# Paged attention: heads 0 and 4 of a batch scored in full precision, heads 1, 2, 3, 5, 6 and 7 in three rounded products

## The reference, cut to what matters

```
B, S, D, HQ, HK = 32, 32, 128, 32, 8      # batches, tokens, head size, query heads, key heads
kc = k_cache[block_table].reshape(B, 512, HK, D)     # 16 pages of 32 keys a batch
k_all = concatenate([kc, k], axis=1)                 # 544 keys
scores = einsum('bqhd,bkhd->bhqk', q, repeat(k_all, HQ // HK, axis=2)) * D ** -0.5
scores = where(valid, scores, -1e30)
o = einsum('bhqk,bkhd->bqhd', softmax(scores), repeat(v_all, HQ // HK, axis=2))
```

## Time and profile before

| | us |
|---|---|
| median of 3 runs (1693.58 to 1695.39) | 1694.57 |
| the profiled execution, its own time | 1689.82 |
| its span, first to last instruction | 1687.6 |
| of it the paged attention, from the first scores to the last values | about 859 to 1475 |

### The profile page before, as it was taken

The page is one execution under the profiler, slowest core; times in us unless marked ns, Lnnn a source line. Parts: engine busy times, 40 slices in busy tenths (PEclk is TensorE's granted clock), DMA queues, the critical chain, the costliest instruction groups (busy, mean ns, idle before and its releaser), DMA issues. The chain is left out here.

```text
span 1687.6 us, 34168 instructions
## 1 busy us (share of the span) xinstructions
PE 1619.2 (96%) x10792; PEld 1404.1 (83%) x10792; DVE 1104.5 (65%) x2942; ACT 943.1 (56%) x2392; POOL 369.9 (22%) x370
## 2 busy tenths in 40 slices
PE   2899999999999999999979999999999999999998
PEld 2787888888888788888869999999999999977777
DVE  8405543454436657777768888888888888864443
ACT  3224323232222266766669989998899888822221
POOL 1000000000000246656532332223222322122210
PEclk9999999999999999999979999999999999999999
DMA  6621121110110433443578889988998898594301
GB/s 231 206 91 52 65 69 68 68 44 24 68 63 26 162 107 107 134 134 106 156 268 277 282 297 300 305 287 286 304 302 295 273 301 299 184 325 140 122 12 50
DMA packets 239311, 290.69 MB, mean 172 GB/s; under 512 B 18682, under 2 KB 182938, under 8 KB 239258
## 3 DMA queue, kind: packets, MB, share of 16 engines
q1 hardware_dynamic: 220826, 222.89, 39.8%
q0 software_dynamic: 18432, 67.12, 12.3%
HBM read 237.43 MB, written 50.41 MB: 171 GB/s over the span
## 5 line engine op out<-in xcount | busy, mean ns | idle before, releaser
L1591 PE MATMUL p_val<-probs_t,vals 128*128 128x128 f32 x2048 | 271.7, 276 | 1.7 <-DMA vals<-in_v_pages,rows_now 1.7
L1591 PEld LDWEIGHTS p_val<-probs_t,vals 128*128 128x128 f32 x2048 | 249.3, 192 | 2.0 <-DMA vals<-in_v_pages,rows_now 2.0
L1501 DVE CUSTOM_DVE_ANT_0 probs<-p_score,mask 128x544 f32<-128x544 f32 x256 | 184.3, 720 | 80.2 <-issue 77.6
L1406 ACT ACTIVATE probs<-probs,low 128x544 f32<-128x544 f32 x256 | 190.6, 745 | 0.3 <-DVE low L1501 0.3
L1060 POOL TENSOR_TENSOR w_lo<-w_raw,w_hi 128x512 fp32r<-128x512 f32 x44 | 57.7, 1316 | 548.4 <-DVE w_hi L1098 531.9
L1414 ACT ACTIVATE probs_t<-p_turn 128x512 f32<-128x512 f32 x256 | 149.5, 584 | 50.6 <-PE p_turn L1570 46.6
L450 PE MATMUL p_score<-wo_hi,q_hi 128*128 128x288 f32 x448 | 153.4, 342 | 11.9 <-DVE low L1501 11.3
L1490 DVE TENSOR_TENSOR wo_lo<-keys,wo_hi 128x544 fp32r<-128x544 f32 x224 | 161.7, 722 | 0.7 <-issue 0.7
L450 PE MATMUL p_tile<-w_hi,y_hi 128*128 128x512 f32 x384 | 156.9, 409 | 2.4 <-PEq L463 2.4
L1570 PE MATMUL p_turn<-cst,probs 128*128 128x128 f32 x1024 | 154.8, 274 | 3.2 <-issue 1.5
L1401 ACT ACTIVATE wo_hi<-keys 128x544 fp32r<-128x544 f32 x224 | 146.1, 652 | 17.6 <-PE p_score L452 12.9
(11 more groups left out here) (216 smaller groups left out, 3604.4 us busy)
## 6 DMA issues: line engine op xcount, KB each, us to landing
keys<-in_k_pages SPq DMA_DIRECT2D x512, 128.0 KB
qk_new<-x_res SPq DMA_DIRECT2D x80, 256.0 KB, 2.3
x_res<-qk_new SPq DMA_DIRECT2D x32, 512.0 KB
o_new<-x_res SPq DMA_DIRECT2D x32, 512.0 KB
w_raw<-in_w_vkq_t SPq DMA_DIRECT2D x12, 1024.0 KB, 5.6
w_raw<-in_w_qkv_t SPq DMA_DIRECT2D x10, 1024.0 KB, 8.2
toep<-kpad SPq DMA_DIRECT2D x32, 256.0 KB, 4.9
w_raw<-in_w_dense_t SPq DMA_DIRECT2D x8, 1024.0 KB, 5.3
```

The lines of the kernel that those rows point to most:

```text
L1406: nc.scalar.activation(probs[:, i % 8, :], probs[:, i % 8, :], ACT.Exp, bias=low[:, i % 4:i % 4 + 1], scale=-1.0, accum_out=total[:, i % 4 ...
L1501: v.tensor_tensor_reduce(out=probs[:, i % 8, :], in0=score_at(i % 2, slice(0, KEYS)), in1=mask[:, i // HK, :], scale=1.0, scalar=3e38, op0 ...
L1591: mm = pe.matmul(p_val[:, h, half * P:(half + 1) * P], vals[:, slot, c, k * D:(k + 1) * D], probs_t[:, i % 2, c, :], start=(c == 0 and hal ...
```

## The change

Head 4 of every batch is treated as head 0 is: `PLAIN = (0, HK // 2)`. `split_hi` and `split_lo` return at once for it, PE takes its scores in two full-precision matmuls from `queries` and `keys`, and doesn't wait for `q_lo` or `k_lo` there. The second piece of the queries, now 384 columns for heads 5 to 7, is split at k = 5. A batch has six splits where it had seven, and `splits_to` counts accordingly.

```diff
--- before.py
+++ after.py
@@ -1305,9 +1305,10 @@
         score_at = lambda n, part: p_score[:, FROM[n] + part.start:FROM[n] + part.stop]
         half_heads = lambda a, slot, n: a[:, slot, n * HQ * S // 2:(n + 1) * HQ * S // 2]
 
-        QUERY_AT = {1: slice(P, HQ * S // 2), HK // 2: slice(HQ * S // 2, HQ * S)}
-        SPLITS = HK - 1
-        splits_to = lambda m, i: 2 * SPLITS * m + i // HK * SPLITS + i % HK
+        PLAIN = (0, HK // 2)
+        QUERY_AT = {1: slice(P, HQ * S // 2), HK // 2 + 1: slice(HQ * S // 2 + P, HQ * S)}
+        SPLITS = HK - len(PLAIN)
+        splits_to = lambda m, i: 2 * SPLITS * m + i // HK * SPLITS + i % HK - (i % HK > HK // 2)
         both = lambda body, eng: (body(0, True), _loop(eng, 1, B // 2, lambda m: body(m, False)))
 
         block = ctx.enter_context(nc.Block())
@@ -1390,7 +1391,7 @@
             def split_hi(m, i):
                 r = m * RB + i
                 slot, k = i // HK, i % HK
-                if k == 0:
+                if k in PLAIN:
                     return
                 if k == 1:
                     act.wait_ge(kq_in[slot], LOADS * m + LOADS)
@@ -1541,15 +1542,15 @@
                 end, middle = ENDS[i % 2], MIDDLES[i % 2]
                 if k == 0:
                     pe.wait_ge(kq_in[slot], LOADS * m + LOADS)
-                else:
+                elif k not in PLAIN:
                     if k in QUERY_AT:
                         pe.wait_ge(q_lo_ready, 4 * m + 2 * slot + (1 if k == 1 else 2))
                     pe.wait_ge(k_lo_ready, splits_to(m, i))
 
                 def product(part):
-                    if k == 0:
-                        return pe.matmul(score_at(i % 2, part), queries[:, slot, 0:P],
-                                         keys[slot][:, part.start // S:part.stop // S, 0, :], start=True, stop=True)
+                    if k in PLAIN:
+                        return pe.matmul(score_at(i % 2, part), queries[:, slot, k * P:(k + 1) * P],
+                                         keys[slot][:, part.start // S:part.stop // S, k, :], start=True, stop=True)
                     return three_pass(pe, score_at(i % 2, part), q_hi[:, slot, k * P:(k + 1) * P], q_lo[:, slot, k * P:(k + 1) * P],
                                       k_hi[:, i % 2, part], k_lo[:, i % 2, part], True, True)
```

## The result

The changed kernel takes 1705.8 us (median, 1703.6 to 1708.7), the kernel before 1695.4 on the same chip (1693.6 to 1697.7): ratio 1.006, 95% interval 1.0044 to 1.0076, 10.4 us more. The forecast was 5.2 us more. The profiled execution of after took 1705.8, its own median; that of before, 1689.82, was faster than any of the runs beside after (1693.6 or more), so that the two traces lie 16 us apart and not 10. I count effects per loop and take times from the medians.

A forecast was written before the change was run, and what follows sets the result against it. PE was taken to bound the paged attention, losing 0.7 us a batch to late reports. 31 x 0.17 = 5.3 us, less some tenths, gave 5.2 on 1689.82: 1695.0 us, range 1693.5 to 1703.0.

The forecast's parts named there:

- PE, head 4, 0.16 us: Full-precision head 4 on PE: 0.16 us more a batch, 32 times, 5.1 us; counts only if the hold's end moves.
- the hold: PE's finished-work reports held up some 1.6 us at head 6 beside POOL's gather; PE loses 0.7 us a batch at head 7.
- `take_values` 0.19 us later, and the hold's end with it: On ACT, queries now split ahead of `take_values` delay it 0.19 us; the hold's end moves 0.17 a batch, bounds 0 and 0.2.
- The relief on ACT and DVE worth nothing: Head 4's rounding on ACT and differences on DVE drop out; neither is in PE's only regular wait, so nothing gained.
- Rival 3: Head 5's report falls into the hold: at least 1.4 us a loop; 1711 in a quarter of loops; chance 0.07.
- The base: Starting time for the whole kernel: one profiled execution, 1689.82 us, giving 1695.0; the same 5.2 on the median gives 1699.8.
- Rival 1: The hold swallows head 4's cost, its end hanging on a self-paced gather: 1694.6 us, give or take 0.8; chance 0.22.
- Rival 2: Less DVE work shortens POOL's second gather and the hold: 0.2 a batch, 6 us faster, 1688.4; chance 0.09.

The follow-up runs named there:

- e10: Kernel before with the gathers of all but the first two batches left out, on a chip without late reports: 1667.4 us, ratio 0.9993.
- e11: Changed kernel with the gathers of all but the first two batches left out, on a chip without late reports: 1674.0 us, ratio 1.0031.
- e4: Kernel before with POOL starting the gather three heads later: 1718.4 us, ratio 1.0141.
- e5: Changed kernel with POOL starting the gather three heads later: 1722.6 us, ratio 1.0162.
- e1: Kernel before, head 4 still rounded, only the queries of heads 5 to 7 split at k = 5: 1705.1 us, ratio 1.0057.
- e8: Kernel before with one more small POOL instruction ahead of each batch's gathers, nothing else moved: 1696.4 us, ratio 1.0015.
- e2: Changed kernel (plain head 4), but queries of heads 5 to 7 split at head 4 as before: 1765.9 us, ratio 1.0416.
- e9: Changed kernel with head 3 plain in place of head 4 and queries split at head 4 as before: 1773.2 us, ratio 1.0457.
- e15: Unaltered copy of e13, run on a chip where PE's reports are late: 1757.2 us, ratio 1.0364.
- e16: Unaltered copy of e12, run on a chip where PE's reports are late: 1766.1 us, ratio 1.0431.
- e7: Changed kernel with each batch's store issued one batch later, behind the key loads: 1695.6 us, ratio 1.0008.
- e13: e2 with one more small POOL instruction ahead of the gathers, on a chip without late reports: 1671.4 us, ratio 1.0022.
- e12: e9 with one more small POOL instruction ahead of the gathers, on a chip without late reports: 1673.5 us, ratio 1.0030.

## Why the prediction was wrong

- *PE, head 4, 0.16 us:* the size is right: 0.15 a loop without a hold (e10, e11), 4.2 us or 0.14 a loop by the medians with late gathers (e4, e5). With the hold in its place it adds nothing to the short loops (19.17 against e1's 19.20), since it stands between `take_values` and the end of the hold; the forecast had it so.
- *`take_values` 0.19 us later, and the hold's end with it:* right. 2.23 us against the forecast 2.24, and from e8 to e1 the short loop grows by 0.15, where I took 0.17. The last late report comes at T+6.5 to 6.7 in either kernel.
- *The relief on ACT and DVE worth nothing:* as far as shown. e1, without it, has ratio 1.0057, the changed kernel 1.006.
- **The step that failed** is the one in front of these: that the hold begins behind head 5, as it did. I priced its end and took its beginning as given. Rival 3 came true, in nearly every loop and not in a quarter of them, and by another way. I had head 5 come 0.16 later into a hold that stood still. Against the `values` of head 7, on which POOL waits, it does come 0.15 later. But the first gather starts 0.25 later against them, because POOL's first small instruction begins earlier in DVE's subtraction and takes 0.52 in place of 0.27, and `take_values` comes 0.17 later. So head 5's scores, at T+2.97 and T+2.99 before, stay where they were against `take_values`, and the gather is at T+0.47 in place of 0.38. That is enough: e1 has the loss with no plain head, and e8 the catch with nothing but the gather moved. A gather that starts later brought a hold that begins earlier; the forecast priced no move of the beginning at all.
- *Rival 3's price,* at least 1.4 us per caught loop, was too much. It is 0.17 in a short loop and about 0.9 in a long one (e8). With the moved queries the loops cost 0.29 and 1.00 more than before: 18 x 0.29 + 12 x 1.00 = 17.2 us, about what the traces differ by (16.8 between the first and the last `take_values`). I had both reports come together at the end of the hold, with two operations of DVE (1.4 us) between them. Head 5's came at T+4.2 to 4.9 and not at 6.6, so DVE had masked it and split the keys by the time that head 6's came; in the rows above the mask of head 6 follows 1.94 behind, and PE stops once.
- *The base:* the forecast hung on one profiled execution that was the fastest of its kernel. The medians differ by 10.4 and the traces by 16, so the usual execution of the kernel before must lose some 5 us more than the one in its trace. Whether that is more caught loops no trace shows. That one trace also had the warning: head 5 held by 0.4 us in three loops, and by 1.34 in the loop with the gather at T+0.50. The forecast read a stretch without them. Its 31 loops are 30; the last interval has no gather.
- *Rival 1* is right for head 4 alone, as far as the short loops show it, and wrong for the queries. *Rival 2:* the second gather got 0.1 shorter and nothing was won. Where it gets really short (e2, e9, e15, e16), the time goes up by 62 to 79 us, the opposite of what rival 2 said.

What stays open is why PE's reports are late beside a gather at all, why on two of the four chips that were met and not on the others, and why a gather at T+0.47 brings an early beginning, one at 0.38 a late one and a third gather at 2.8 an early one again with the longest waits. Open too is what makes a caught loop short or long, and with it the largest part of the loss: by the traces the 12 longer loops of the changed kernel cost 0.7 us each on top, 8.5 us. They come with the later `take_values` and the store in its place (e8 and e7 have one and none). A shorter store, which would have told its share, was not tried.

## What to carry to other kernels

A wait that appears in the profile without a releaser, while the producer was long done, was a late report here: look at what else runs then (here an indirect DMA), and price both its ends against every instruction near them, since 0.15 us in a gather's start alone put another head into the hold (e8), 0.1 us together with a copy 0.17 us later went with 10 us (e1), and 0.6 us in the third one's with over 60 (e15, e16). Before a term of 0.3% is believed, take more than one execution and more than one chip; here the choice of chip is worth 25 us and the change 10 where there is a hold, and some 5 where there is none by kernels near it (e10 and e11, e13). A change that only moves work still moves the DMAs that wait on it: compare their places against each other, not only the work's.

## What the runs showed of the hardware

- The same program takes 1694 us on some chips and 1668 on others. What differs is late reports of PE beside the gathers: without gathers the kernel takes 1670.7 on a chip with holds and 1667.4 on one without.
- POOL's gather instruction and DVE's work hold each other up. In e16 the records show DVE's subtraction starting just ahead of the second gather in every loop in which that gather is in its place: by 0.044 to 0.045 us in the 7 where the gather then takes 1.49, and by 0.030 to 0.043 in the 22 where it takes 0.94 and the subtraction 0.79 to 0.80. That looks like an order of arrival, with the turning point between; it is inferred from these starts. The Trainium skill says in SBUF — State Buffer, section "SBUF: two separate sides", that the port pair that DVE and GpSimd share goes whole to the one that starts first; for a DVE operation with two SBUF inputs it says so only where the GpSimd operation reads SBUF. The trace agrees in kind: the subtraction has two such inputs, the gather reads its row numbers from a tile in SBUF, and the one that is late takes 0.55 or 0.07 us longer.
- In e16 which of the two wins goes with the fate of head 5 in all 29 loops: where DVE kept POOL waiting for 0.55 us the loop took 1.3 to 3.9 us less. On a chip without holds it made no difference (e12).
